# Scaling the expert weights on ScalarE instead of GpSimd, in an attention and mixture-of-experts kernel

## The reference

```python
def xattn(x, c, w_proj, b_proj):            # x is layer-normed
    q = x.reshape(B, T, H, d) * scale; k = c.reshape(B, S, H, d) * scale; v = c.reshape(B, S, H, d)
    w = softmax(einsum('bthd,bshd->bhts', q, k), axis=-1)
    return einsum('bhts,bshd->bthd', w, v).reshape(B, T, W) @ w_proj.T + b_proj

def ffn(x, Wg, W1, W2, W3):                  # x is layer-normed, hidden size 682
    logits = einsum('bsd,ed->bse', x, Wg)
    gating = softmax(where(in_top_2, logits, -inf))
    h1 = einsum('bsd,ehd->bseh', x, W1); h2 = einsum('bsd,ehd->bseh', x, W2)
    out = einsum('bseh,edh->bsed', silu(h1) * h2, W3)
    return einsum('bsed,bse->bsd', out, gating)

x = x + xattn(layernorm(x), ctx, ...)
x = x + ffn(layernorm(x), ...)
```

## Time and profile before

| | us |
|---|---|
| median of 3 runs | 897.08 |
| lowest and highest | 895.11, 900.03 |
| the profiled execution | 896.09 |
| its span, first to last instruction | 894.3 |
| busy in the span: PE, DVE, ACT, POOL | 786.5, 603.1, 541.7, 467.7 |
| mean granted TensorE clock | 0.978 |

### The profile page before, as it was taken

The page is one execution under the profiler, slowest core; times in us unless marked ns, Lnnn a source line. Parts: engine busy times, 40 slices in busy tenths (PEclk is TensorE's granted clock), DMA queues, the critical chain, the costliest instruction groups (busy, mean ns, idle before and its releaser), DMA issues.

```text
span 894.3 us, 19943 instructions
## 1 busy us (share of the span) xinstructions
PE 786.5 (88%) x6344; PEld 476.9 (53%) x6344; DVE 603.1 (67%) x1258; ACT 541.7 (61%) x938; POOL 467.7 (52%) x432
## 2 busy tenths in 40 slices
PE   0478888989989898888989899997999999999995
PEld 0112223323322332232237688886888888888884
DVE  4788988979979799799715557553555555555552
ACT  3258779878878887868773445452444444444442
POOL 4566357787878978787623665222333222222222
PEclk9999999989989999999989999998999999999998
DMA  8584666939378384865283969999996879483832
GB/s 171 139 223 148 207 131 214 198 107 272 120 258 177 134 238 144 226 160 185 91 278 141 240 183 286 286 276 212 265 262 160 203 210 260 76 242 55 245 48 24
DMA packets 109794, 167.51 MB, mean 187 GB/s; under 512 B 58656, under 2 KB 87072, under 8 KB 105120
## 3 DMA queue, kind: packets, MB, share of 16 engines
q1 hardware_dynamic: 96288, 148.77, 59.4%
q0 software_dynamic: 13440, 17.90, 10.6%
HBM read 119.75 MB, written 42.55 MB: 181 GB/s over the span
## 4 chain that ended last, share of the span: by engine, by line
PE 58%; POOL 12%; ACT 7%; SPq 7%; issue 6%; DMA 3%; DVE 2%; POOLq 0%; ACTq 0%; DVEq 0%
PE ps L1376 9%; PE ps L1378 9%; PE ps L1380 9%; PE ps L1304 8%; POOL slots L474 5%; ACT probs L846 5%; PE ps L1394 4%; PE ps L1396 4%; PE ps L1289 4%; PE ps L1398 4%; PE ps L1276 3%; SPq L622 3%; POOL w_lo L763 2%; POOL w_in L752 2%; DVE neg_max L974 1%
## 5 line engine op out<-in xcount | busy, mean ns | idle before, releaser
L974 DVE TENSOR_REDUCE neg_max<-ps 128x2 f16<-128x1024 f32 x256 | 307.5, 1222 | 36.2 <-PE ps L1276 32.7
L846 ACT ACTIVATE probs<-ps 128x1024 f32<-128x1024 f32 x256 | 257.5, 1026 | 80.6 <-PE ps L1289 76.7
L773 POOL DMA_INDIRECT out<-y,aim x72 | 112.6, 1564 | 249.4 <-DVE y L1207 163.7
L1376 PE MATMUL ps<-zt,w 128*128 128x256 f16 x792 | 217.8, 275 | 7.2 <-DMA w<-w_parts 5.8
L1378 PE MATMUL ps<-zt,w 128*128 128x256 f16 x792 | 217.7, 275 | 0.0
L1380 PE MATMUL ps<-zt,w 128*128 128x256 f16 x792 | 217.6, 275 | 0.0
L875 ACT ACTIVATE silu<-ps 128x256 f32<-128x256 f32 x216 | 82.5, 382 | 193.1 <-PE ps L1380 189.2
L1188 DVE SCALAR_TENSOR_TENSOR hid<-ps,silu 128x256 f32<-128x256 f32 x216 | 91.8, 425 | 143.4 <-ACT silu L875 139.8
L1276 PE MATMUL ps<-k_stack,q_stack 48*128 48x512 f16 x512 | 105.5, 410 | 50.4 <-ACT probs L846 31.7
L1304 PE MATMUL ps<-probs,v_ext 128*32 128x512 f32 x1024 | 139.9, 618 | 4.7 <-ACT heads L909 3.7
L1289 PE MATMUL ps<-q_stack,k_stack 49*128 49x512 f16 x512 | 102.0, 397 | 12.8 <-DVE neg_max L974 6.4
(11 more groups left out here) (126 smaller groups left out, 963.8 us busy)
## 6 DMA issues: line engine op xcount, KB each, us to landing
w<-w_parts SPq DMA_DIRECT2D x36, 1408.0 KB
w<-w_parts SPq DMA_DIRECT2D x36, 768.0 KB
w_in<-in_w SPq DMA_DIRECT2D x16, 704.0 KB
v_ext<-in_v SPq DMA_DIRECT2D x8, 1024.0 KB, 6.4
k_stack<-k SPq DMA_DIRECT2D x48, 128.0 KB, 6.8
q_stack<-qt SPq DMA_DIRECT2D x48, 128.0 KB, 7.9
w_in<-in_w SPq DMA_DIRECT2D x8, 768.0 KB
w_parts<-w_hi SPq DMA_DIRECT2D x16, 352.0 KB, 2.6
```

The source lines that it names most:

```text
L773: nc.gpsimd.indirect_dma_start(out=out, out_offset=bass.IndirectOffsetOnAxis(ap=aim[frm][:, t, 0:1].bitcast(U32), axis=0), in_=y[frm][:, t ...
L846: nc.scalar.activation(probs[g % 2][:, j:j + 2, k, :], pair_banks[PLACE["exp", u] % 3], ACT.Exp, scale=0.25).then_inc(s_exp, 1)
L974: nc.vector.tensor_reduce(neg_max[b % 2][:, g, c:c + 9:8], pair_banks[PLACE["max", u] % 3], AX.X, ALU.max, negate=True).then_inc(s_red, 1)
L1376: nc.tensor.matmul(dst, w[:, kk, 1, cols], z16[:, kk, :], start=(kk == 0), stop=False)
```

## The change

The multiplication by 256 moves from POOL to ACT, as an ACTIVATE with a scale, in place on `w_in`. ACT has it at slots 1, 6 and 12, behind the second exponential unit of the slot, and waits there for the load. POOL's `split_weights` starts with the rounding, once ACT has signalled `s_wsc`. `s_wop` now counts one per chunk. The constant tile `scale_w` and its memset are gone. The loads, their order and SP's program stay as they were.

```diff
+AT_W_SCALE = (1, 6, 12)
...
-        scale_w = sb("scale_w", [P, 1])
...
+        s_wsc = sem("s_wsc")
...
-                sp.wait_ge(s_wop, n * 2 + 2)
+                sp.wait_ge(s_wop, n + 1)
...
-            sp.wait_ge(s_zero, 4)
+            sp.wait_ge(s_zero, 3)
...
-            nc.gpsimd.memset(scale_w[:, :], WSCALE).then_inc(s_zero, 1)
...
                 x, hi, lo = w_in[:, 0:size], w_hi[:, 0:size], w_lo[:, 0:size]
-                pool.wait_ge(s_wld, (n + 1) * 16)
-                nc.gpsimd.tensor_tensor(x, x, scale_w[:, 0:1].to_broadcast([P, size]),
-                                        ALU.mult).then_inc(s_wop, 1)
-                pool.wait_ge(s_wop, n * 2 + 1)
+                pool.wait_ge(s_wsc, n + 1)
                 ge(pool, s_wst, n * 32)
                 nc.gpsimd.tensor_copy(hi, x).then_inc(s_whi, 1)
...
+                for c, off in enumerate(AT_W_SCALE):
+                    for e in due(slot, off):
+                        size = UP if c < 2 else HC * W
+                        act.wait_ge(s_wld, (e * 3 + c + 1) * 16)
+                        nc.scalar.mul(w_in[:, 0:size], w_in[:, 0:size], WSCALE).then_inc(s_wsc, 1)
                 for b in due(slot, AT_K_HI):
```

More of the change, by code:

```diff
@@ L679, in _ @@
                 nc.gpsimd.memset(k_stack[i][:, :, :].bitcast(F32), ONES_PAIR).then_inc(s_zero, 1)
-            pool.wait_ge(s_zero, 4)
+            pool.wait_ge(s_zero, 3)
             def inverse_root(agg, rs, sh, done, b):
@@ L1412, in _ @@
                     pe.wait_ge(s_bias, K_BIAS)
-                    pe.wait_ge(s_zero, 4)
+                    pe.wait_ge(s_zero, 3)
                 scores_st(slot, 0)
```

## The result

The changed kernel takes 906.89 us (median of 21 runs, 901.81 to 917.40) and the kernel before, on the same chip, 900.25 us (21 runs, 892.81 to 909.61). The ratio is 1.0084, interval 1.0064 to 1.0104: slower by some 7 us. A second set of runs on another chip gives 903.45 against 898.41, 1.0066 (1.0035 to 1.0098). Medians here are of all runs, ratios only of the fast ones (at most 1.5% above the fastest of the same kernel), so a ratio differs a little from the quotient of the medians beside it.

A forecast was written before the change was run, and what follows sets the result against it. PE, DVE and ACT were taken as 80 to 90% busy, with POOL narrowly on the path. Relief -4.4, costs +19.0, load +1.2 and maxima -1.4 gave +14.4 on 896.1, forecast 910 us, range 899 to 919.

The forecast's parts named there:

- the base: Whole kernel: the profiled execution's 896.09 us before the change, to which the forecast added its sum of +14.4 us.
- the relief: Windows 3 to 6: without POOL's scale, z_n's root comes 2.55 us earlier and ACT's four waits go, -4.4 us.
- the maxima's -1.4: Slot 16: PE's waits for row-maximum DMAs absorb chunk 2's delays, 0.7 us each in windows 1 and 6.
- 1.2 for the load: Chunk 1, windows 3 to 6: ACT waits 0.3 us per window for w_in, holding up queued work; +1.2 us.
- The costs, 19.0 us: 24 scales on ACT at slots 1, 6 and 12 delay PE and ACT; the delays sum to 19.0 us.
- the faster rival: Windows 3 to 6: POOL sets the pace and the scales fall in ACT's idle time; 889 us, chance 0.10.
- My bound of 3 in all: Changed kernel's profile: ACT's wait for w_in was to stay under 3 us in all.
- No difference (898): Half of the delay is made up later, where ACT waits for PE; 898 us, chance 0.12.
- Much slower (922): w_in lands behind ACT's place in chunk 1 of windows 3 to 7 and some chunk 2; 922 us, chance 0.10.

The follow-up runs named there:

- the first profile: The first profiled execution of the change, unedited: 917.40 us, 10.5 over its median.
- the second profile of the change: The changed kernel run again without edit on another chip, 903.45 us against 898.41 for the kernel before; its profiled execution took 908.26 us.

## Why the prediction was right and wrong

The direction held: slower, by 5 to 7 us against my sum of 14.4, and 906.9 us lies in the range. The sum was too high by 7 to 9, and that the number came out within 4 of the forecast is in part luck, by the base. By the ratios of the experiments, at 898 us, the three chunks can be set beside the terms of the forecast:

| | forecast | measured |
|---|---|---|
| chunk 0, with the relief | -4.4 + 4.6 + 0.4 = +0.6 | -4.0 |
| chunk 2 added, with the maxima's -1.4 | +4.2 | +4.1 |
| chunk 1 added, with 1.2 for the load | +9.6 | +5.7 to +7.4 |
| sum | +14.4 | +5.9 to +7.5 |

Each ratio is known to 0.3 to 0.4%, so a row is known to some 3 to 4 us. Only the first row's difference, 4.6, is clear of that; that chunk 1's cost was too high is likely but not shown. The second row's agreement may be chance: its -1.4 is open (below), and waits for the load lie in what was measured.

**The base.** I added to 896.1. The same kernel has a median of 900.25 over 21 runs, so the profiled execution was a lucky one (the later sets have 896.9 to 898.6). From that median my +14.4 would have given 914.7. The base hid half of the error of the sum.

**The costs, 19.0 us: right to about 2 us.** By the slots, +0.64 at slot 1 (I had 0.65), +1.27 at slot 6 (1.28), +0.65 at slot 12 (0.7). Summed over the windows where I had them, the slots give 18.0: 3.9 for chunk 0 (windows 1 and 7 make up more, 0.24 and 0.48 remain), 8.3 for chunk 1, 5.8 for chunk 2. Of the last, 1.3 are in window 0, where PE in this execution still ran at half clock, up to 71.0 us; in the first profile, where that ended at 63.5, it is 0.4, so that some 17 are the places' own. One ACTIVATE took 1.37 or 1.48 us (1.38, 1.49). Windows 1 and 2 say the same: window 2 grew by 4.0, 0.64 + 1.27 + 0.65 = 2.56 of it in the three places (I had forecast 2.6), and 1.5 at slot 8 from a half clock. That the places are not ACT's gaps, my argument against the faster rival, is what decided: PE did wait 1.27 us more behind slot 6.

**ACT's wait for w_in, +1.2: not where I had it.** Chunk 1 in windows 3 to 6 never waits for its load in either profile of the change. Chunk 2 does once, 1.8 us in window 3 of the first profile, and with the clock behind it this costs 4.1 us; how often that happens no run shows. The page's 5.0 us is one other wait, for the second load of window 0, at 43.44, ahead of the first exponential at 47.6. My bound of 3 in all missed that one, and it costs nothing that I can find: the first exponential came at 48.8 before the change.

**The relief, -4.4: half of what it was.** This is the step that failed. I priced the stall at z_n by ACT's waits alone. The slots give 4.9, and the half clock behind PE's matching wait 4.0 more; the kernel that scales nothing gains 10.5 in these windows and 10.9 by the medians (interval 6 to 13 us, without my 4.4 in it). The mean clock rises by 0.004 to 0.007 in every kernel that takes chunk 0's scale off POOL without putting chunk 1's on ACT, an estimated 2 to 5 us. I had the evidence in the earlier trace rows, a granted clock of 0.94 in window 3 against 1.00 in window 5, and set it aside since window 3 seemed only 0.5 us longer. It was 2.5 longer: I had let window 5's stretch run 2 us into window 6. One start time read wrongly took away nearly half of the gain.

**What I did not see coming.** The new wait of PE at slot 7 can bring a half clock of its own, 1.5 us each in windows 2, 3 and 6 of the second profile, none in the first. In the pair of profiles that I compare it is as much clock as the removed stall gave back. On average it is less: the mean clock of the change, 0.980 and 0.982, is above the 0.977 of before, so the change gains by the clock and loses by the places. It is in none of my cases.

**The -1.4 for the maxima's DMAs: open.** Slot 15 of windows 1 and 6 takes 4.03 and 4.78 in the one profile of before, 2.90 and 4.84 in the other, 4.21 and 3.53 in the second profile of the change, 5.27 and 6.14 in the first. That spread is larger than the term.

**The balance.** Between the profiles: -4.9 (slot 5), -4.0 (clock before), +18.0 (the three places), +4.4 (clock now, slots 7 and 8) is +13.5, against 12.9 at the last exponential of attention and 12.0 at the end of the span. The profile of the changed kernel lies above its median and that of before below, so that the medians' +5 to +7 is the better number. By the medians alone, scaling nowhere gains 10.9 and ACT's scales give back 15.9. By the mean clocks, little of the 15.9 and some 3 of the 10.9 are clock. The places' 17 less the relief's 4.9 is +12 before any clock, and the medians have +5 to +7; the mean clock explains an estimated 2 to 3 us of that gap. What else an average execution of before loses that its profiled one does not stays open, since only single executions have a trace.

**The rivals.** No difference (898) had its mechanism, made-up delays, refuted: in windows 2 to 6 the next slots make up nothing beyond what I had counted. Faster (889) needed under 0.15 us per scale, and the change has 0.64 to 1.27; but its point on the clock was right, and its time is what chunk 0 in a real gap gives. Much slower (922) needs w_in late in most windows, as in the kernel with chunk 1 alone; the first profile of the change, 917.40, has it once, in chunk 2.

## What to carry to other kernels

Here, moving work off an engine paid for the one piece that stood ahead of a critical hand-over, chunk 0, and paid most (8 us against 4) where the new owner had it in a gap: place each piece by itself, and move no more than is needed. Test a removed stall by a kernel that leaves the work out before pricing the rest. Price a stall by what the next engines do behind it, its clock included, and not by the wait alone. Before comparing stretches, cut them at the same event; an error of 2 us in 55 is enough to hide the effect.

## What the runs showed of the hardware

TensorE's granted clock fell from 2.4 to 1.2 GHz behind single waits of PE of 1.3 to 1.75 us between busy stretches (196.0 and 250.6 in the one profile of before, 355.1 in the other, 210.9 with chunk 0 at slot 3), and behind one of 2.50 (230.8 in the first profile of the change). One stretch behind the shorter waits cost 1.4 to 2.0 us here. The same wait did not always bring it: in windows 4 and 5 of the second profile of the change, at 263.27 for one, the clock stayed at 1.00, and so it did behind the 1.32 and 1.50 us of windows 5 and 6 before (PE starting at 305.75 and 359.15).

An ACTIVATE with a constant scale on 128x1408 in SBUF took 1368 ns in the mean of 16, and one on 128x1536 1475. In the prediction I had weighed a surcharge of 93 ns for a pointer operand from the Trainium skill, "ScalarE: Activation LUTs", What ACT_TABLE_LOAD costs; that section's form without one gives 186 + 0.833 x 1408 = 1359 ns (an estimate from that page), and 1466 for 1536. The trace agrees with both to 10 ns: there was no surcharge.
